# Cross-attention with a routed low-rank projection: x laid out transposed by the host, mean subtracted there, rstd applied in the exponential

## What is computed

```python
def _layernorm(x, axis=-1, eps=1e-05):
    return (x - mean(x)) / sqrt(var(x) + eps)

def _L0_xattn_ref(query, key):
    a = einsum('bqd,bkd->bqk', query, key)
    e = softmax(a, axis=-1)
    return einsum('bqk,bkd->bqd', e, key)

x = x + _L0_xattn_ref(_layernorm(x), ctx_4096)
x = x + _L0_ffn_ref(_layernorm(x), base_w, base_b, A, B, router_w)
```

## Time and profile before

| what | value |
|---|---|
| median of 3 runs | 1385.78 us (1384.99 to 1386.0) |
| the profiled execution: its own time | 1386.35 us |
| its span, first to last instruction | 1384.6 us |
| PE busy | 1347.0 us, 97% of the span, 6777 matmuls |
| DVE busy | 941.5 us, 68% |
| ACT busy | 625.5 us, 45% |
| POOL busy | 306.6 us, 22% |
| DMA | 345.34 MB, mean 249 GB/s |
| mean granted TensorE clock | 0.996 of full speed |

### The profile page before, as it was taken

How to read it: one execution, slowest core, us unless ns; L and a number is a source line. 1 busy time by engine, 2 the same in 40 slices (tenths; PEclk the granted TensorE clock), 3 DMA queues, 4 the chain that set the end, 5 groups by cost and what they waited for, 6 DMA issues and landing times.

```text
span 1384.6 us, 17941 instructions
## 1 busy us (share of the span) xinstructions
PE 1347.0 (97%) x6777; PEld 1103.0 (80%) x6777; DVE 941.5 (68%) x1193; ACT 625.5 (45%) x777; POOL 306.6 (22%) x233
## 2 busy tenths in 40 slices
PE   5999999999999999998999999999999999999998
PEld 4778788887878888886888877887878888888886
DVE  6587778788777778868466467777776564555554
ACT  3355555645565555545421366767775211111010
POOL 2002002020201102020614733444442111111110
PEclk9999999999999999999999999999999999999999
DMA  8968778788877868779656698999984977888784
GB/s 294 296 219 265 218 256 247 229 258 258 281 225 248 265 218 257 237 241 220 209 173 178 188 278 258 313 328 297 327 252 153 342 249 249 275 247 274 245 260 148
DMA packets 160248, 345.34 MB, mean 249 GB/s; under 512 B 51680, under 2 KB 68064, under 8 KB 145760
## 3 DMA queue, kind: packets, MB, share of 16 engines
q1 hardware_dynamic: 141600, 277.06, 64.6%
q0 software_dynamic: 10528, 52.85, 12.0%
q10 hardware_dynamic: 8064, 14.68, 2.9%
HBM read 260.87 MB, written 99.41 MB: 260 GB/s over the span
## 4 chain that ended last, share of the span: by engine, by line
PE 42%; DMA 7%; DVE 3%; issue 1%; ACT 1%; POOL 0%; SPq 0%; POOLq 0%; DVEq 0%
PE scores L887 13%; PE scores L889 13%; PE scores L888 13%; DMA y_scratch<-y_out,yrow_i 5%; PE work L923 2%; PE work L924 2%; DMA a_in<-xT_scratch 1%; DVE a_l L1464 1%; DVE raw_l L1217 1%; DMA res<-x_scratch 0%; DVE w_l L1455 0%; DVE x L1252 0%; DMA hs_scratch<-hg,pos_i 0%; POOL hs_scratch L1680 0%; ACT y_out L1115 0%
## 5 line engine op out<-in xcount | busy, mean ns | idle before, releaser
L887 PE MATMUL scores<-w_h,a_h 128*128 128x512 f32 x896 | 352.6, 393 | 4.0 <-issue 3.2
L889 PE MATMUL scores<-w_h,a_l 128*128 128x512 f32 x896 | 351.8, 393 | 0.0
L888 PE MATMUL scores<-w_l,a_h 128*128 128x512 f32 x896 | 351.3, 392 | 0.0
L1091 ACT ACTIVATE a_h<-a_in 128x512 fp32r<-128x512 f32 x148 | 83.5, 622 | 319.4 <-DMA a_in<-xT_scratch 210.6
L887 PEld LDWEIGHTS scores<-w_h,a_h 128*128 128x128 f32 x896 | 168.9, 188 | 41.8 <-issue 3.6
L889 PEld LDWEIGHTS scores<-w_h,a_l 128*128 128x128 f32 x896 | 168.7, 188 | 38.0
L888 PEld LDWEIGHTS scores<-w_l,a_h 128*128 128x128 f32 x896 | 168.8, 188 | 37.1
L1217 DVE TENSOR_TENSOR raw_l<-raw_in,val_h 128x512 fp32r<-128x512 f32 x192 | 155.4, 827 | 47.1 <-ACT val_h L1017 46.4
L753 PE MATMUL scores<-ctxT_h,nT_h 128*112 128x494 f32 (+1 forms) x512 | 174.0, 340 | 1.1 <-DVE nT_l L1203 1.1
L755 PE MATMUL scores<-ctxT_h,nT_l 128*112 128x494 f32 (+1 forms) x512 | 171.5, 335 | 0.0
L754 PE MATMUL scores<-ctxT_l,nT_h 128*112 128x494 f32 (+1 forms) x512 | 171.4, 335 | 0.0
(11 more groups left out here) (151 smaller groups left out, 1983.6 us busy)
## 6 DMA issues: line engine op xcount, KB each, us to landing
ctxT_in<-in_ctxT_dram SPq DMA_DIRECT2D x64, 750.0 KB, 7.7
raw_in<-in_ctx_dram SPq DMA_DIRECT2D x32, 1280.0 KB
a_in<-xT_scratch SPq DMA_DIRECT2D x37, 1024.0 KB, 7.5
w_in<-in_wT_dram SPq DMA_DIRECT2D x32, 512.0 KB, 8.6
x<-in_x_dram SPq DMA_DIRECT2D x8, 1792.0 KB, 9.5
y_add<-y_scratch SPq DMA_DIRECT2D x56, 256.0 KB, 5.8
late_y<-y_scratch SPq DMA_DIRECT2D x56, 256.0 KB, 6.5
xn<-in_x_dram SPq DMA_DIRECT2D x7, 1792.0 KB, 15.4
```

The source lines that it names most:

```text
L887: pe.matmul(o, ah, wh, start=(k == 0), stop=False)
L888: pe.matmul(o, ah, wl, start=False, stop=False)
L889: last = pe.matmul(o, al, wh, start=False, stop=(k == KD - 1))
```

## The change

The host also gives xT, x of each batch transposed as [128, 16, 224]. For batches 1 to 7 the 32 transposes of xn are gone, and so is ACT's normalisation of xn; batch 0 stays as it is. The tiles xn and x2 become a pair `rows`, used in turn: the raw rows of batch b + 1 are loaded once, into the tile of batch b - 1, and serve for the statistics and later for the residual. xT is loaded into xT_in, the memory of nT_l. SP stores the mean and variance of the rows (mv1, 16 bytes on each of 112 partitions) to memory, waits, and loads them spread over 128 partitions. DVE subtracts the mean from xT_in in four groups (`centre`); ACT and DVE split them (`x_high_part`, `x_low_part`). The scores are then those of x - mean; rstd multiplies the negated maximum (one more instruction of two columns, with a wait for the maximum) and is the scale of the exponential.

Where the work goes: the eight statistics of the next rows all stand at e = 4 to 7, two each, the mean at e = 8. Groups 0 and 1 of xT are centred at e = 13 and 17, their high parts follow at e = 15 and 19, their low parts at e = 16 and 20; groups 2 and 3 are centred behind ctx_low(2) and ctx_low(4) of the next batch and split beside blocks 3 and 5. ctx_low(1) of the next batch moves from ahead of the last residual to behind the first four of the eight statistics of x2. On SP the load of the next rows stands where x was loaded; xT's load waits for the hidden product, and the mean's store and load follow it, ahead of the values of c = 0 and all that stands behind them. In the last batch the first four w loads go from behind the first x2T group to behind the last. On PE, ACT and DVE the loop over the mid batches is written out.

```diff
-LN1_AT = (9, 10)
-QT_AT = (13, 14, 16, 17)
+STATS_AT = (4, 5, 6, 7)
+MEAN_AT = 8
+CENTRE_AT = (13, 17)
+X_HIGH_AT = (15, 19)
+X_LOW_AT = (16, 20)
...
-            nT_l = sb("nT_l", [P, KD, LQ], F32R, first)
+            nT_l, xT_in = sb_in("nT", [P, KD, LQ], first)
...
+        rows = [xn, x2]
+        mean_in = bias_b[:, 0, 0:2 * LQ]
...
+            def load_row(b):
+                sp.dma_start(rows[b % 2][:, :, :], x_v[b]).then_inc(row_loaded[b % 2], 16)
+            def load_xT(b):
+                sp.dma_start(xT_in[:, :, :], xT[b]).then_inc(xT_loaded, 16)
+            def spread_mean(b):
+                sp.wait_ge(aggr1, b * NQ + NQ)
+                sp.dma_start(mean_d[b], mv1[:, :, :]).then_inc(mean_stored, 16)
+                sp.wait_ge(mean_stored, b * 16)
+                at_least(sp, centred, (b - 1) * NX)
+                sp.dma_start(mean_in, mean_d[b].rearrange("p q s -> (p q s)").unsqueeze(0).to_broadcast([P, 2 * LQ])).then_inc(mean_loaded, 16)
...
-                if last:
-                    sp.wait_ge(filled, job_no("last", b, "x2T", 0))
-                    for j in range(PAIRS // 2):
-                        load_w(j)
                 if not last:
                     if first:
+                        load_row(1)
                         sp.wait_ge(filled, job_no("pre", 0, "qT", NX - 1) + 1)
-                    else:
-                        sp.wait_ge(filled, job_no("mid", b, "x2T", 0))
-                    sp.dma_start(xn[:, :, :], x_v[b + 1]).then_inc(xn_loaded, 16)
+                        sp.dma_start(xn[:, :, :], x_v[0]).then_inc(xres_loaded, 16)
...
                     sp.wait_ge(filled, job_no(stage, b, "x2T", NX - 1) + 1)
-                sp.dma_start(x2[:, :, :], x_v[b]).then_inc(xres_loaded, 16)
                 if not last:
+                    if not first:
+                        load_row(b + 1)
                     score_done(sp, b, NPC - 1)
                     load_ctxT(b + 1, LR - 1)
+                    if not first:
+                        sp.wait_ge(filled, job_no(stage, b, "hid") + 1)
+                        sp.wait_ge(xT_staged, b * NX)
+                    load_xT(b + 1)
+                    spread_mean(b + 1)
                     raw_again(b, 0)
                 else:
+                    for j in range(PAIRS // 2):
+                        load_w(j)
...
-                    if stage != "last" and e in QT_AT:
-                        pe.wait_ge(ln1_done, b * NQ + NQ)
-                        transpose_rows(stage, b, "qT", xn, QT_AT.index(e))
...
-                               scale=1.0, accum_out=rsum[:, q:q + 1]).then_inc(exp_done, 1)
+                               scale=1.0 if b == 0 else rs1[:, q:q + 1],
+                               accum_out=rsum[:, q:q + 1]).then_inc(exp_done, 1)
+            def x_high_part(b, n):
+                act.wait_ge(centred, (b - 1) * NX + n + 1)
+                act.activation(four_blocks(nT_h, n), four_blocks(xT_in, n), ACT.Copy).then_inc(x_high, 1)
...
+                dve.reduce_max(nraw[:, q:q + 1], all_scores(q), AX.X, negate=True).then_inc(max_step, 1)
+                dve.wait_ge(rstd1, b + 1)
+                dve.wait_ge(max_step, (b - 1) * NQ + q + 1)
+                dve.tensor_tensor(nmax[:, q:q + 1], nraw[:, q:q + 1], rs1[:, q:q + 1],
+                                  ALU.mult).then_inc(max_ready, 1)
+            def centre(b, n):
+                if n == 0:
+                    dve.wait_ge(xT_loaded, b * 16)
+                    dve.wait_ge(mean_loaded, b * 16)
+                cut = slice(4 * n, 4 * n + 4)
+                four = xT_in[:, cut, :].rearrange("a k (q p) -> a k q p", q=NQ)
+                dve.tensor_tensor(four, four, mean_b.unsqueeze(1).to_broadcast([P, 4, NQ, QT]),
+                                  ALU.subtract).then_inc(centred, 1)
+            def x_low_part(b, n):
+                dve.wait_ge(x_high, (b - 1) * NX + n + 1)
+                dve.tensor_tensor(four_blocks(nT_l, n), four_blocks(xT_in, n), as_f32(four_blocks(nT_h, n)),
+                                  ALU.subtract).then_inc(x_ready, 1)
...
+                    if old and j == 1:
+                        ctx_low(b, 1)
...
                         for i in range(4 * j, 4 * j + 4):
-                            stats(x2, st2, stat2, i)
+                            stats(rows[(b - 1) % 2], st2, stat2, i)
...
+                    if old and j in (2, 4):
+                        centre(b, 2 + (j - 2) // 2)
+                    if old and j in (3, 5):
+                        x_low_part(b, 2 + (j - 3) // 2)
...
                 if new:
-                    for j in range(HR):
-                        ctx_low(b + 1, j)
+                    ctx_low(b + 1, 0)
                 residual(b, CH - 1)
...
-            with dve.Fori(1, NB - 1) as b:
+            for b in range(1, NB - 1):
                 one(b, "mid")
```

More of the change, by code:

```diff
@@ L162, in xattn_ffn_kernel @@
         "pre": group("qT", NX),
-        "first": group("eT", NQ) + group("qT", NX),
-        "mid": BEFORE + group("eT", NQ) + OLD + group("qT", NX),
+        "first": group("eT", NQ),
+        "mid": BEFORE + group("eT", NQ) + OLD,
         "last": BEFORE + group("eT", NQ) + OLD,
@@ L358, in xattn_ffn_kernel @@
         x_first = [sem(f"x_first{c}") for c in range(CH)]
-        xn_loaded = sem("xn_loaded")
+        row_loaded = [sem(f"row_loaded{i}") for i in range(2)]
+        xT_loaded = sem("xT_loaded")
+        mean_stored = sem("mean_stored")
+        mean_loaded = sem("mean_loaded")
+        centred = sem("centred")
+        x_high = sem("x_high")
+        x_ready = sem("x_ready")
+        max_step = sem("max_step")
         xres_loaded = sem("xres_loaded")
@@ L763, in scores_of @@
                     pe.wait_ge(ctx_ready, b * NPC + j + 1)
-                    if stage == "first" and j % 2 == 0:
-                        pe.wait_ge(drained, job_no("pre", 0, "qT", j // 2) + 1)
+                    if j % 2 == 0:
+                        if stage == "first":
+                            pe.wait_ge(drained, job_no("pre", 0, "qT", j // 2) + 1)
+                        else:
+                            pe.wait_ge(x_ready, (b - 1) * NX + j // 2 + 1)
                     ks = range(CP * j, CP * j + CP)
@@ L852, in outputs_of @@
                         out = scores[0:QT, (c + 1) % 2, q * BANK:(q + 1) * BANK]
-                        rows = rows_of(t)
-                        eh, el = eT_h[0:rows, q, t, :], eT_l[0:rows, q, t, :]
-                        vh, vl = val_h[0:rows, e % NR, :], raw[0:rows, c, t, :]
+                        used = rows_of(t)
+                        eh, el = eT_h[0:used, q, t, :], eT_l[0:used, q, t, :]
+                        vh, vl = val_h[0:used, e % NR, :], raw[0:used, c, t, :]
                         pe.matmul(out, eh, vh, start=(t == 0), stop=False)
@@ L949, in _ @@
             one(0, "first")
-            with pe.Fori(1, NB - 1) as b:
+            for b in range(1, NB - 1):
                 one(b, "mid")
@@ L1015, in value_high @@
                     act.wait_ge(raw_loaded[c], b * 32 + 32)
-                rows = rows_of(t)
-                act.activation(val_h[0:rows, e % NR, :], raw_in[0:rows, c, t, :],
+                used = rows_of(t)
+                act.activation(val_h[0:used, e % NR, :], raw_in[0:used, c, t, :],
                                ACT.Copy).then_inc(val_high, 1)
@@ L1027, in one @@
                     ctx_high(b, j)
+                    if stage != "first" and j in (3, 5):
+                        x_high_part(b, 2 + (j - 3) // 2)
                     if stage == "first" and j in (2, 3):
@@ L1121, in _ @@
             one(0, "first")
-            with act.Fori(1, NB - 1) as b:
+            for b in range(1, NB - 1):
                 one(b, "mid")
@@ L1215, in value_low @@
                 dve.wait_ge(val_high, b * (CH * NT) + e + 1)
-                rows = rows_of(t)
-                dve.tensor_tensor(raw[0:rows, c, t, :], raw_in[0:rows, c, t, :], as_f32(val_h[0:rows, e % NR, :]), ALU.subtract).then_inc(val_ready, 1)
+                used = rows_of(t)
+                dve.tensor_tensor(raw[0:used, c, t, :], raw_in[0:used, c, t, :], as_f32(val_h[0:used, e % NR, :]),
+                                  ALU.subtract).then_inc(val_ready, 1)
             def stats(tile, st, sem_stat, i):
@@ L1407, in one @@
                     x2T_low(NX - 1)
-                if new and old:
-                    dve.wait_ge(xn_loaded, b * 16 + 16)
-                    for i in range(4):
-                        stats(xn, st1, stat1, i)
                 for q in range(NQ):
@@ L1437, in one @@
                         tile_low(0, (FIRST_A_AT.index(e),))
-                    if new and e - 3 in QT_AT:
-                        n = QT_AT.index(e - 3)
-                        low(stage, b, "qT", n, four_blocks(nT_h, n), four_blocks(nT_l, n), 2, 2 * LQ)
                     if c >= 1 and t == 3:
```

69 lines of the change are left out of this document (37 added, 32 removed).

## The result

The changed kernel takes 1396.87 us, the median of 7 runs (1393.92 to 1398.6), beside 1385.78 for the kernel before in the same series (7 runs, 1383.28 to 1390.73). The ratio is 1.0061, with a 95% interval of 1.0043 to 1.008: slower by more than 0.2%. The forecast was 1380.9, slightly faster; the range of 1372 to 1403 holds the time. The profiled execution took 1398.6 us with a span of 1396.9, against 1386.35 and 1384.6, so 12.3 us more. I compare these two.

A forecast was written before the change was run, and what follows sets the result against it. PE was taken to bound the attention batches, with DVE second. The terms -21.6 + 11.2 - 1.2 + 3.0 + 3.0 + 0.7 = -4.9 us gave 1380.9 us against the median of 1385.78, range 1372 to 1403.

The forecast's parts named there:

- a, transposes: Outputs of seven stages: 28 groups of eight PE transposes gone, 0.77 us each, 21.6 us less.
- 0.2 a batch that I gave eT_l: Before the outputs: eT_l ends earlier as four statistics leave its front; 0.2 less in six batches, 1.2 us less.
- b, ctx_low(1): Scores, batches 1 to 7: PE waits 1.73 at block 1 for ctx_low(1) behind four statistics; net 11.2 us more.
- The gain at block 2: Scores: ctx_low(2) is done before PE wants it, so the present 0.2 wait at block 2 goes.
- c, the centring: Centring and splitting x on DVE and ACT: 1.03 us per centring, upper end 1.2; no wait in the scores, zero.
- d, the outputs: Outputs of batches 1 to 6: PE waits 0.3, and 0.2 at step 18; 0.5 x 6 = 3.0 us more.
- lower end: Mean's trip through memory by fastest store and load, 2.4 and 3.0: back at 238.3, due 239.1; upper end 244.3.
- e, batch 0: Batch 0, step 14: mean's store behind xT on a full queue, wait 3.1, clock loss 1.2, -1.3: 3.0 us more.
- f: The rest: last batch's w loads moved and x load gone, 0.7 us more; written-out loops and SP's later stores zero.
- the late mean of my rivals: Step 14 waits for the mean, each us costing six over the batches: 1416 at upper ends, 1398 half way; chance 0.20.
- The others: Rivals: SP's queue 1393 (0.10); block 1 not late 1369.7 (0.07); batch 0 without wait 1376.6 (0.10); no effect 1402.5 (0.05).

The follow-up runs named there:

- Experiment 7: Changed kernel with block 1's low part ahead of the last residual again, the mean spread for batch 1 alone and no centring: 1369.24 us, ratio 0.9872.
- experiment 6: Changed kernel with the mean spread once, for batch 1, and the centring replaced by an instruction that does nothing: 1378.37 us, ratio 0.9915.
- experiment 9: Changed kernel plus one DVE copy per batch of the spread means into a dense tile that the centrings read: 1387.17 us, ratio 0.9984.
- Experiment 5: Changed kernel with the mean stored and spread once; batches 2 to 7 subtract batch 1's mean, all DVE instructions kept: 1382.22 us, ratio 0.9958.
- experiment 10: Changed kernel with block 1's low part early again, and centring and splitting of groups 0 and 1 behind later output steps: 1376.17 us, ratio 0.9909.
- experiment 1: Changed kernel with ctx_low(1) put back ahead of the last residual: 1384.21 us, ratio 0.9964 to the kernel before.
- experiment 8: Changed kernel with, in batch 0 alone, the load of x transposed issued behind the mean's load: 1393.51 us, one run.
- experiment 3: Kernel before with only the mid-batch loops of PE, ACT and DVE written out: 1382.86 us, ratio 0.9948.

## Why the prediction was wrong

**a, transposes, -21.6: right.** Experiment 7 gives 3.10 in the outputs of a batch against 4 x 0.77 = 3.08. It also shows nothing of the 0.2 a batch that I gave eT_l: with all costs away the outputs start 42.5 us after the scores, as before (42.55; 42.38 with the loops written out). A miss of 1.2.

**b, ctx_low(1), +11.2: right.** 1.67 at block 1 (forecast 1.73), 11.1 when undone, 1.6 in each mid batch when done alone. The gain at block 2 came as well.

**c, the centring at 1.03: the first step that failed.** It takes 1.78. The instruction's length was not the question: for the same 896 elements the low part of x, with plain operands, takes 1.08. I looked at how many elements it reads and not at how they lie, though the diff shows the access pattern, one word in four. I had called the scores safe up to 1.2, with 0.45 us to spare at block 4; it was block 3 that came late. The length alone does not do it: by the forecast's own sum ctx_low(3) would still end at 188.4 + 0.6 + 1.78 + 1.72 = 192.5, before block 3 is due at 192.7. The rest is a wait that the prediction left out, DVE's 0.59 for rstd. POOL's rs takes 0.69 us where nothing runs beside it (experiment 6), 1.46 beside a centring of 1.08 (experiment 9) and 2.18 beside one of 1.79:

```profile
190.97 0.69 POOL L1679 TENSOR_TENSOR rs<-ve,mhalf 112x2 f32<-112x2 f32 x1 [31.71 <-DVE ve L1264]
```

```profile
191.81 1.46 POOL L1684 TENSOR_TENSOR rs<-ve,mhalf 112x2 f32<-112x2 f32 x1 [33.20 <-DVE ve L1265]
```

```profile
196.12 2.18 POOL L1680 TENSOR_TENSOR rs<-ve,mhalf 112x2 f32<-112x2 f32 x1 [33.83 <-DVE ve L1263]
```

In all three it starts 0.25 us after DVE's ve, and beside a centring it ends some 0.55 after the centring does. So the centring holds up the next ctx_low by its length and by POOL's delay together. In the scores this cost about 0.4 a batch, so that they are 2.05 longer in place of 1.4. No run moves the one without the other.

**d, the outputs at +0.5 a batch: the step that decided.** A mid batch's outputs last 36.24 us on average, against 36.75 - 3.08 = 33.67: +2.6. Over six batches that is 12.4 us more than forecast, three quarters of the miss in batches 1 to 6 (16.4). The times up to the mean were right: aggregated 11.5 us after the start of the outputs, as forecast (232.6 - 221.06; 241.74 - 230.26). Then my two numbers left no slack: the mean back at 17.2 after that start, due at 18.0. It was back at 18.3, as the trip took 6.8 us from the statistics in place of 5.7, and with the longer centring it was due at 17.3. I took each at its lower end; one of them at its middle would have used up the 0.8 us. The trip itself varies (6.3 to 7.4 us from the store's issue to the centring, 9.3 in batch 3), and the delay then runs on to step 18, which I had at 0.2 and which is 0.83. Experiment 5 shows that the trip is the cause (13.1 in S), experiment 9 that the centring's length adds to it, experiment 10 that later centrings remove nearly all of the waits in the outputs (36.1 to 33.9), at 1.0 or more in the scores.

The lower end came from the fastest 256 KB store and load. The store was even faster (1.8 in the median against 2.4), but the load took 4.1 to 6.2 against 3.0. The Trainium skill (DMA: Bandwidth & Descriptors, Anatomy of one DMA) has 2.0 us fixed for a DMA on GpSimd's path. The store, issued by SP, took 1.4 to 1.8 in four of the six mid batches, somewhat less, and 3.0 and 3.2 in the other two; for the load, 224 KB read out of 1.8 KB of memory, its sum of about 2.5, an estimate, is too low by two.

**e, batch 0 at +3.0: too small.** Its distance grew by 3.9 where I had -0.1 with the transposes in; experiment 1, whose batch 0 is the same up to its end, has one of 82.4, so the size is uncertain by some 2 us. PE wants step 14 at 80.9 as forecast, but that is luck: the outputs began 2.2 later (61.22 against 59.03), and a lower clock that had cost the kernel before some 1.6 at their start (windows below) did not come this time. It gets step 14 at 87.9 in place of 84.0: the store, behind x transposed, landed 1.9 later (80.9, forecast 79), the load took 1.4 longer (4.6, forecast 3.2), the centring 0.7. The loss by the clock came too, twelve matmuls at nearly twice the spacing (0.43), some 2.5 us where I had 1.2. The two windows, from the start of batch 0's outputs in the kernel before and in the changed one:

```profile
59.00:64.00 5.00, 4.96 (x15) 3.69 (x16) 1.37 (x3) 0.97 (x2) 0.00 (x0) 0.66 1.03 319
```

```profile
61.20:66.20 5.00, 4.98 (x22) 3.76 (x23) 2.64 (x5) 1.77 (x3) 0.00 (x0) 1.00 1.03 249
```

That the store stands behind x transposed was right, and experiment 8 shows it. The Trainium skill (the same page, Queues, rings and completion order) says that each DMA engine takes a ring's descriptors in order; 9.1 behind and 3.5 ahead agree.

**f and the projection.** The last batch is +0.6 over before where I had +2.3 (1.6 of b and 0.7 of f). Here costs that I added overlap: its score part is 2.2 longer, and while PE waits there the first tile of a arrives, so that the wait at step 10 of its outputs falls from 1.9 to 0.25. The projection half was 2.7 shorter in this profile; other runs with the same code there differ as much.

By parts, from the profiled runs: start of the program +1.2, batch 0 +3.9, batches 1 to 6 +9.3 (forecast -7.1), batch 7 +0.6, projection -2.7; together 12.3 for the span. The case is the late mean of my rivals, with a chance of 0.20: the mechanism stood there with the right place, and at 1398 half way. That 1398 lies so near the measured time is partly luck: that rival had neither the longer centring nor the wait at block 3, the last batch came out 1.7 below its forecast, and the projection half 2.7 shorter. The others did not come: PE never waited for ctxT_h's load in the changed kernel, and the freed PE time is not lost to a full DVE (experiment 5, where DVE has all its instructions and the outputs still take 33.7 to 34.5).

## What to carry to other kernels

Moving work off the bound pays what the spacing of its instructions says, but only if no result that replaces it is due at the very moment it is ready. Count the slack of each new trip and of each moved instruction, and where it is under a microsecond, place the consumer later: here the same work, put in a better order and with one small copy that closes the gaps between the means, went from 0.6% slower to 1.5% faster, each beside the kernel before in its own series. Price an elementwise instruction by how its operands lie as well as by their number.

## What the runs showed of the hardware that was not expected

- **A gap in one operand.** An fp32 subtraction of 128x896 in SBUF takes 1.78 us when one operand is read 16 bytes apart, and 1.09 when it is dense. The Trainium skill (Advanced Engine Details and Errata, SBUF Cachelines) says that reads which hit a new line of 16 bytes each time are slower; the trace agrees, with 64% more here. A copy of 128x224 out of the same gaps took 0.36; what a dense one takes was not measured.
- **A small POOL instruction beside a DVE one.** POOL's rs, 112x2, took 0.69 us with nothing beside it, 1.46 beside a subtraction of 1.08 on DVE and 2.18 beside one of 1.79 (spans on POOL are rough, but DVE's wait of 0.59 for it is measured on DVE).
- **Tiny pieces.** 1.8 KB in 112 pieces of 16 bytes are in memory after 1.8 us in the median, half as many bytes in 224 pieces of 4 after 6.2.
- **The clock behind a pause.** PE's pauses of 2.9 and 6.9 us in the outputs were followed by granted clocks of 0.64 and 0.50 for 4 to 5 us, and cost 1.5 and 2.5 more; matmuls of 512 columns then stood 0.43 apart in place of 0.23, the spacing of the 1.2 GHz level. The length of the pause alone does not decide it. At step 14 of batch 3 a pause of 2.75 in experiment 9 was followed by 0.64 over the next 3.9 us, one of 2.70 in experiment 1 by 1.00; and the same two pauses of 1.3 and 1.7 ahead of batch 0's outputs were followed by the lower clock in the kernel before and in experiment 1, but not in the changed kernel.
- **Loops written out** made mid batches 0.17 us shorter, not longer (experiment 3).
